# Attention's output in a fused macaron kernel: division on GpSimd, early value chunks and an early attention share, output products that accumulate both parts

## The chip, the cores and the metric

The kernel runs on one core of one Trainium2 chip. The metric is the device time of one execution in microseconds. A core has four engines that compute (TensorE, VectorE, ScalarE, GpSimd) and a queue that only issues transfers (SyncE); each works through its own list of instructions in order, and semaphores tie the lists together. In the rows below they are PE (PEld is its loading of weights), DVE, ACT, POOL and SP.

## What is computed

The reference has three stages on x of 4 batches x 1024 tokens x 128 channels: a local-attention stack of two layers, one global attention with a line memory, and the same local stack again. The change is in the end of the middle stage:

```python
attn = jax.nn.softmax(scores, axis=-1)
seq_out = jnp.einsum('bhts,bhsd->bhtd', attn, v)
...
mem_val = x @ memv_w.T + memv_b
gate = jax.nn.sigmoid(x @ memg_w.T + memg_b)
mem_score_t = jnp.transpose(mem_score, (0, 2, 1))
gated = jax.nn.sigmoid(mem_score_t * mem_scale) * gate
gated = jnp.mean(gated, axis=-1, keepdims=True)
return (seq_out + gated * mem_val) @ out_w.T + out_b
```

`x` in these lines is the normalised input, `y` in the kernel; the result is added to the residual stream, `x` in the kernel. All of this is fp32.

## The kernel before

`macaron_kernel` runs a setup pass, `local_attention_pass`, `global_attention_pass` and `local_attention_pass` again. A barrier of all engines stands between two passes, so the second local pass starts when the slowest engine of the global pass is through. All tensors are laid with channels on the partitions and tokens along the row.

**The global pass** ends with the line memory, a loop over 8 tiles of 128 tokens (`body(t)` in each engine's list, t = 0 to 7, all four batches at once). For tile t TensorE makes `memory(t, 0)` to `memory(t, 5)` (16 heads of 144 columns, line 1821), into three PSUM banks in turn; VectorE multiplies each bank by the read lines (`terms`, 2044), sums (`read_memory`, 2054), and makes the score of the tile in three steps (`weigh`, 2062, 2066, 2070); TensorE turns the score to rows (`turn`, 1830), and ScalarE copies it out (`copy_scores`, 2396). In tiles 0 to 5 TensorE also makes the lines of tile t + 2; tiles 6 and 7 have none, so they are short. Tile 6 is `body(LAST - 1)`, tile 7 is `body(LAST)`; `turn(6)` is the last step of `body(7)`, and `turn(7)` is all of `body(8)`.

**The output stage** works on 8 chunks of 512 tokens; chunk i is batch i % 4, half i // 4. For each chunk:

- `memory_value` (1857): memv x y, one fp32 product of 128x512; ScalarE adds the bias (`value_bias`, 2410).
- the spread inverse of the softmax's sums, a product of 32 rows (1873), and the spread mean of the gate, a product of 16 rows (1879). `inverse_and_mean(pair)` makes both for two chunks: four products on four different quarters of TensorE's rows.
- VectorE: `scale_seq` (2106) is the attention's sum times the inverse, `gate_value` (2113) the value times the mean.
- GpSimd: `combine` (2309) adds the two.
- TensorE: `back` (1885), out_w x the combined chunk, one product; VectorE adds the bias and the residual (`back`, 2121).

The gate needs, once for each half, `gates` (1844, four products of 16 columns side by side), two sigmoids on ScalarE (2399, 2404) and a product on GpSimd (`gate_product`, 2302). Half 1 needs the scores of all tiles, and with them `turn(7)`.

The order is written out by hand in each list. On TensorE: `gates(0)`, `gates(1)`, `memory_value(0)` and `(1)` after tile 6; `inverse_and_mean(0)` inside tile 7; `memory_value(2)` and `(3)` behind it; and the rest behind `turn(7)`. The banks of lines and tails (M0 to M0 + 2, O0) are free from tile 6 on, the memory's banks (S0 to S0 + 3) after tile 7.

## Time and profile before

| | us |
|---|---|
| median of 3 runs | 1919.88 (1919.46 to 1920.75) |
| profiled execution | 1922.61 |
| its span, first to last instruction | 1920.7 |
| tiles 6 and 7, `memory(6, 3)` to `turn(7)` | 1228.24 to 1243.01 |
| `turn(7)` to the last VectorE instruction of the stage | 1243.01 to 1264.55 |

The rows that stand further down come from this one profiled execution. Times in them are counted from the start of its span. A matmul in fp32 leaves two records in the trace, so a product of 128x512 is "x2" there. A row of the timeline merges neighbours of one kind: its duration runs from the start of the first record to the end of the last.

### The profile page before, as it was taken

The numbers are of one execution on the slowest core, as the hardware profiler recorded it, in microseconds if no ns is written. First come the engines' busy times: TensorE is split into PE (matmuls) and PEld (weight loads), VectorE is DVE, ScalarE is ACT, GpSimd is POOL, SyncE is SP. The second block draws the span as 40 slices with busy tenths as digits, with TensorE's granted clock in tenths as the row PEclk, the third lists the DMA queues.
The fourth block names the chain that finished last, engine by engine and source line by source line (L and its number), as shares of the span: only waits on it lengthen the run. The fifth ranks groups of instructions, "written<-read, shape, count | busy, mean of one in ns | idle before, by whom it ended". The sixth has DMA issues, their size and how long they took to land. (4 is left out here: it accounts for less than half of the span.)

```text
span 1920.7 us, 61287 instructions
## 1 busy us (share of the span) xinstructions
PE 1856.6 (97%) x22646; PEld 1108.6 (58%) x22646; DVE 1603.5 (83%) x5443; ACT 1491.9 (78%) x4110; POOL 929.2 (48%) x568
## 2 busy tenths in 40 slices
PE   7999999999999989999999999889999999999999
PEld 3777774577775443344444448637777635777754
DVE  5899974899995668999999949979999658999945
ACT  4999995699998362777777763469999847999973
POOL 2788861488883050000000036648888405888820
PEclk9999999999999995999999999999999999999999
DMA  6212230122221041111111000002121201222211
GB/s 179 50 44 50 45 70 6 29 47 48 47 54 42 1 151 38 42 41 41 42 41 41 26 7 5 2 20 51 44 51 44 62 6 36 45 50 45 67 23 44
DMA packets 76330, 85.33 MB, mean 44 GB/s; under 512 B 17327, under 2 KB 50803, under 8 KB 75907
## 3 DMA queue, kind: packets, MB, share of 16 engines
q1 hardware_dynamic: 75839, 81.40, 17.0%
q8 instruction: 182, 2.98, 0.7%
q14 instruction: 113, 0.93, 0.2%
q10 hardware_dynamic: 196, 0.02, 0.0%
HBM read 20.83 MB, written 8.39 MB: 15 GB/s over the span
## 5 line engine op out<-in xcount | busy, mean ns | idle before, releaser
L336 ACT ACTIVATE probs<-probs,negmax 128x128 f32<-128x128 f32 x1024 | 401.9, 402 | 2.3 <-DVE negmax L411 1.9
L2328 ACT ACTIVATE gprobs<-ps_global 128x1024 f32<-128x1024 f32 (+3 forms) x384 | 291.5, 811 | 126.2 <-PE ps_global L1765 103.5
L291 POOL TENSOR_TENSOR rot<-rot 128x1024 f32<-128x1024 f32 x128 | 302.5, 2363 | 143.9 <-DVE rot L381 143.9
L297 POOL TENSOR_TENSOR qk<-rot,cnorm 128x1024 f32<-128x1024 f32 x128 | 244.0, 1906 | 173.6 <-issue 150.9
L304 POOL TENSOR_TENSOR probs<-probs,iden 128x1024 f32<-128x1024 f32 x128 | 243.0, 1898 | 47.2 <-DVE iden L419 46.5
L2010 DVE TENSOR_REDUCE maxes<-ps_global 128x1 f32<-128x512 f32 (+2 forms) x384 | 222.1, 639 | 11.6 <-PE ps_global L1728 6.5
L411 DVE CUSTOM_DVE_ANT_0 probs<-ps_attn,masks 128x128 f32<-128x128 f32 x1024 | 226.2, 287 | 0.8 <-issue 0.8
L336 ACT ACTIVATION_READ_ACCUMULATOR probs<-probs,negmax 128x1 f32 x1024 | 204.2, 199 | 0.0
L1723 PE MATMUL ps_global<-kq 48*128 48x512 bf16 (+3 forms) x768 | 197.3, 346 | 7.1 <-DVE maxes L2010 1.8
L2240 POOL CAST m_parts<-m_turn 32x128 bf16<-32x128 f32 x16 | 4.5, 282 | 364.7 <-DVE m_turn L2024 364.7
L377 DVE TENSOR_TENSOR rot<-ps_attn,rotary 128x512 f32<-128x512 f32 x256 | 175.1, 684 | 1.8 <-PE ps_attn L202 1.5
L1780 PE MATMUL ps_global<-gprobs,v_all 128*9 128x512 f32 (+3 forms) x1536 | 161.3, 492 | 1.0 <-ACT gprobs L2328 1.0
L271 PEld LDWEIGHTS ps_attn<-probsT,v_first 128*64 128x64 f32 x2048 | 103.8, 137 | 97.7 <-ACT probsT L357 93.9
L255 PEld LDWEIGHTS ps_attn<-ident,probs 128*128 128x128 f32 x1024 | 120.4, 142 | 67.0 <-issue 64.6
L638 ACT ACTIVATE ln<-ps_attn,vecs_sb 128x512 f32<-128x512 f32 (+2 forms) x96 | 65.6, 684 | 115.7 <-PE ps_attn L600 71.6
L387 DVE TENSOR_REDUCE ssq<-sq 128x16 f32<-128x1024 f32 x128 | 154.8, 1209 | 0.1
L2006 DVE CUSTOM_DVE_ANT_0 ps_global<-ps_global,later 128x384 f32<-128x384 f32 (+1 forms) x256 | 152.2, 653 | 2.7 <-PE ps_global L1723 0.6
L1723 PEld LDWEIGHTS ps_global<-kq 48*128 48x128 bf16 x768 | 58.9, 94 | 160.7 <-DVE maxes L2010 86.9
L224 PE MATMUL ps_attn<-ident,qk 128*128 128x128 f32 x1024 | 141.3, 281 | 7.2 <-POOL qk L297 4.4
L1756 PE MATMUL ps_global<-kq 51*128 51x512 bf16 (+3 forms) x768 | 145.6, 330 | 2.7 <-ACT gprobs L2328 1.9
L282 PE MATMUL ps_attn<-oT,wo_sb 128*128 128x128 f32 x1024 | 135.3, 275 | 0.0
L255 PE MATMUL ps_attn<-ident,probs 128*128 128x128 f32 x1024 | 133.6, 274 | 0.6 <-POOL probs L304 0.6
(235 smaller groups left out, 4501.5 us busy)
## 6 DMA issues: line engine op xcount, KB each, us to landing
v_first<-v_second SPq DMA_DIRECT2D x256, 128.0 KB, 2.3
hs<-z_a SPq DMA_DIRECT2D x256, 32.0 KB, 1.9
ln<-z_b SPq DMA_DIRECT2D x56, 128.0 KB, 2.4
kq<-split_scratch SPq DMA_DIRECT2D x64, 96.0 KB
kq<-split_scratch SPq DMA_DIRECT2D x64, 64.0 KB
split_scratch<-parts SPq DMA_DIRECT2D x8, 384.0 KB, 4.3
split_scratch<-gprobs SPq DMA_DIRECT2D x6, 384.0 KB, 4.0
x_tok<-in_x_dram SPq DMA_DIRECT2D x4, 512.0 KB, 5.8
```

What stands on the lines that cost most here:

```text
L255: last = nc.tensor.transpose(ps[:, b, s * TILE:(s + 1) * TILE], probs[:, k % 2, 4 * e + s, :], K["ident"][:, :])
L291: nc.gpsimd.tensor_tensor(a, a, b, ALU.add).then_inc(C["rot_sum"], 1)
L297: nc.gpsimd.tensor_tensor(qk[:, k % 2, :].rearrange("p (h d) -> p h d", d=DH), rot_a[:, k % 2, :, :], cnorm[:, k % 2, :].unsqueeze(2).to_b ...
L304: nc.gpsimd.tensor_tensor(pr, pr, iden[:, k % 2, :].unsqueeze(2).to_broadcast([P, HEADS, SPAN]), ALU.mult).then_inc(C["probs_ready"], 1)
L336: last = nc.scalar.activation(probs[:, k % 2, slot, :], probs[:, k % 2, slot, :], ACT.Exp, scale=-1.0, bias=negmax[:, k % 2, slot:slot + 1 ...
L377: nc.vector.tensor_tensor(rot_a[:, k % 2, h0:h0 + HEADS, :], x, cos, ALU.mult)
L387: nc.vector.reduce_sum(ssq[:, k % 2, :], sq[:, :].rearrange("p (h d) -> p h d", d=DH), AX_X).then_inc(C["ssq_done"], 1)
L411: nc.vector.tensor_tensor_reduce(probs[:, k % 2, slot, :], ps[:, SB0 + slot // 4, (slot % 4) * SPAN:(slot % 4 + 1) * SPAN], K["masks"][:, ...
L1723: mm = nc.tensor.matmul(out, qs[buf][rows, p, tile_cols(t)], ks[buf][rows, p, CHUNK * c:CHUNK * c + w], start=True, stop=not masked_here, ...
L1780: mm = nc.tensor.matmul(ps[32 * h:32 * h + AD + 1, O0, t0 - CHUNK * c:CHUNK], v_all[:, S_TILES * (n // GROUPS) + s, GROUP * (n % GROUPS) + ...
L2010: nc.vector.reduce_max(maxes[:, n % 2, r, p0:p1, t, c], ps[:, bank_of(use), 0:len(both) * w].rearrange("q (p s) -> q p s", s=w), AX_X).the ...
L2328: nc.scalar.activation(probs[:, step % RING, 2 * p:2 * p + 2, 0:w], ps[:, S0 + 2 * p:S0 + 2 * p + 2, 0:w], ACT.Exp).then_inc(C["p2_exp"], 1)
```

## The change

Per chunk the arithmetic is split differently. GpSimd multiplies the attention's sum by the spread inverse in place (`divide_attention`), after ScalarE has copied that inverse out of PSUM (`copy_inverse`), since GpSimd works on SBUF. `combine` and `scale_seq` are gone. The two parts meet in PSUM instead: `out_w` is multiplied with the divided attention and with the gated value separately.

- For chunks 0 to 3 `attention_part` makes out_w x attention plus identity x residual, and ScalarE writes the sum with the bias to x (`attention_sum`); `back` is then one product, and VectorE adds it to x.
- For chunks 4 to 7 `back` makes out_w x attention and out_w x gated value in one bank; chunks 5 and 7 add identity x residual there too, and ScalarE writes them (`late_sum`).

The inverses are spread in pairs of their own (`inverse_spread`), and the means of a half in one group of four (`means`). A list of 22 names, `EARLY`, gives the order in which the four free banks are used; "V0" is the value of chunk 0, "I" an inverse, "G" a gate, "X" an attention part.

```diff
+        EARLY = ("V0", "V1", "I0", "I1", "V2", "V3", "G0", "G1", "I2", "I3", "I4", "I5", "V4", "V5", "X0", "X1", "I6", "I7",
+                 "X2", "X3", "V6", "V7")
+        FREED = (M0, M0 + 1, M0 + 2, O0)
...
+            def await_early(kind, i):
+                n = early(kind, i)
...
+                wait(pe, "oo_taken", n - 3)
...
+            def inverse_spread(i):
+                b, half = batch_half(i)
+                first = 32 * ((b + 2) % B)
+                await_early("I", i)
...
+                nc.tensor.matmul(ps[:, early_bank("I", i), :], A["head_spread"][first:first + 32, half, :], iden[first:first + 32, :],
+                                 start=True, stop=True, tile_position=(first, 0)).then_inc(C["oo_early"], 1)
...
+            def attention_part(i):
+                await_early("X", i)
+                wait(pe, "oo_norm", i + 1)
+                nc.tensor.matmul(ps[:, early_bank("X", i), :], A["out_w"][:, :], chunk_of(o_all, i), start=True, stop=False)
+                nc.tensor.matmul(ps[:, early_bank("X", i), :], K["ident"][:, :], chunk_of(x, i), start=False, stop=True
+                                 ).then_inc(C["oo_early"], 1)
+
+            def means(half):
+                wait(pe, "oo_prod", half + 1)
+                if half == 0:
                     wait(pe, "ml_term", USES_M * S_TILES)
...
+                for b in range(B):
+                    mm = nc.tensor.matmul(ps[:, mean_bank(b), :], A["head_mean"][32 * b:32 * b + AH, :],
+                                          prod[32 * b:32 * b + AH, half, :], start=True, stop=True, tile_position=(32 * b, 0))
+                mm.then_inc(C["oo_mean"], 1)
...
             def back(i):
-                wait(pe, "oo_comb", i + 1)
-                nc.tensor.matmul(ps[:, inverse_bank(i), :], A["out_w"][:, :], comb[:, i % 2, :], start=True, stop=True
-                                 ).then_inc(C["oo_proj"], 1)
+                await_back_bank(i)
+                out = ps[:, back_bank(i), :]
+                if i < B:
+                    wait(pe, "oo_gated", i + 1)
+                    nc.tensor.matmul(out, A["out_w"][:, :], gated_of(i), start=True, stop=True).then_inc(C["oo_proj"], 1)
+                    return
+                wait(pe, "oo_norm", i + 1)
+                nc.tensor.matmul(out, A["out_w"][:, :], chunk_of(o_all, i), start=True, stop=False)
+                if i in LATE_SUMS:
+                    nc.tensor.matmul(out, K["ident"][:, :], chunk_of(x, i), start=False, stop=False)
+                wait(pe, "oo_gated", i + 1)
+                nc.tensor.matmul(out, A["out_w"][:, :], gated_of(i), start=False, stop=True).then_inc(C["oo_proj"], 1)
...
+            def divide_attention(i):
+                wait(gp, "oo_taken", early("I", i) + 1)
+                nc.gpsimd.tensor_tensor(chunk_of(o_all, i), chunk_of(o_all, i), inverse_of(i), ALU.mult).then_inc(C["oo_norm"], 1)
...
+            def copy_inverse(i):
+                wait(act, "oo_early", early("I", i) + 1)
+                wait(act, "oo_norm", i - 3)
...
+                nc.scalar.copy(inverse_of(i), ps[:, early_bank("I", i), :]).then_inc(C["oo_taken"], 1)
```

VectorE now runs `gate_value` for chunks 0 to 3, `back` 0 to 2, `gate_value` 4 to 7, then `back` 3, 4 and 6. GpSimd divides chunks 0 to 3 behind tile 7's lines, makes `gate_product(0)`, divides 4 to 7, and makes `gate_product(1)`. ScalarE's order from tile 6 on: `copy_scores(4)`, values 0 and 1, `scale_lines(6)`, inverses 0 and 1, values 2 and 3, the first half's sigmoid and both gate sigmoids, inverses 2 and 3, `copy_scores(5)`, inverses 4 and 5, values 4 and 5, `scale_lines(7)`, attention sums 0 and 1, inverses 6 and 7, attention sums 2 and 3, `copy_scores(6)`, values 6 and 7, `copy_scores(7)`, the second half's sigmoid, and the sums of chunks 5 and 7.

TensorE's list between `turn(5)` (16x128 from gprobs) and tile 7's first memory product (v_all, decay), before:

```order
L1830 MATMUL ps_global<-ident,gprobs 16x128 x3
L1844 MATMUL ps_global<-z_a,memg_sb 16x512 [waits ml_state,ml_mul]
L1844 MATMUL ps_global<-z_a,memg_sb 16x512 x7
L1857 MATMUL ps_global<-z_a,memv_sb 128x512 x2
L1821 MATMUL ps_global<-v_all,decay 128x144 [waits ml_term,ml_row1]
```

And now:

```order
L1844 MATMUL ps_global<-ident,gprobs 16x128 x3
L1862 MATMUL ps_global<-z_a,memv_sb 128x512 [waits oo_taken] x2
L1878 MATMUL ps_global<-z_a,memg_sb 16x512 [waits oo_taken]
L1878 MATMUL ps_global<-z_a,memg_sb 16x512 x3
L1878 MATMUL ps_global<-z_a,memg_sb 16x512 [waits oo_taken]
L1878 MATMUL ps_global<-z_a,memg_sb 16x512 x3
L1871 MATMUL ps_global<-later,head_spread_sb 128x512 [waits oo_taken] x2
L1835 MATMUL ps_global<-v_all,decay 128x144 [waits ml_term,ml_row1]
```

A pair of spread inverses now stands there beside two values (chunks 2 and 3; values 0 and 1 moved up into tile 6, with another pair of inverses).

TensorE's list from `turn(6)` to the first `back`, before (`turn(7)` is the second row of ident, gprobs that waits):

```order
L1830 MATMUL ps_global<-ident,gprobs 16x128 [waits ml_out,ml_score]
L1830 MATMUL ps_global<-ident,gprobs 16x128 x3
L1857 MATMUL ps_global<-z_a,memv_sb 128x512 [waits ml_term]
L1857 MATMUL ps_global<-z_a,memv_sb 128x512
L1830 MATMUL ps_global<-ident,gprobs 16x128 [waits ml_out,ml_score]
L1830 MATMUL ps_global<-ident,gprobs 16x128 x3
L1873 MATMUL ps_global<-later,head_spread_sb 128x512 [waits oo_prod,ml_out,oo_stage,oo_value]
```

And now, from behind `turn(6)`:

```order
L1885 MATMUL ps_global<-z_b,out_w_sb 128x512 [waits oo_norm,oo_taken]
L1886 MATMUL ps_global<-x_sb,ident 128x512
L1885 MATMUL ps_global<-z_b,out_w_sb 128x512 [waits oo_norm,oo_taken]
L1886 MATMUL ps_global<-x_sb,ident 128x512
L1871 MATMUL ps_global<-later,head_spread_sb 128x512 [waits oo_taken] x2
...
L1862 MATMUL ps_global<-z_a,memv_sb 128x512 [waits oo_taken]
L1897 MATMUL ps_global<-v_all,head_mean_sb 128x512 [waits ml_out,ml_term,oo_prod]
L1897 MATMUL ps_global<-v_all,head_mean_sb 128x512 x3
L1862 MATMUL ps_global<-z_a,memv_sb 128x512 [waits oo_taken]
L1844 MATMUL ps_global<-ident,gprobs 16x128 [waits ml_out,ml_score,oo_taken]
```

Two values stood between the two turns; now there are eight products of the attention parts (four shown), two values, a pair of inverses and the first half's means.

The end of TensorE's list in this stage, before:

```order
L1873 MATMUL ps_global<-later,head_spread_sb 128x512 [waits oo_prod,oo_x,oo_stage,oo_value]
L1873 MATMUL ps_global<-later,head_spread_sb 128x512
L1879 MATMUL ps_global<-v_all,head_mean_sb 128x512 x2
L1885 MATMUL ps_global<-kq,out_w_sb 128x512 [waits oo_comb] x4
```

And now, behind `means(1)` (chunks 2 and 3 first):

```order
L1916 MATMUL ps_global<-kq,out_w_sb 128x512 [waits oo_gated,oo_taken]
L1916 MATMUL ps_global<-kq,out_w_sb 128x512 [waits oo_gated,ml_out]
L1919 MATMUL ps_global<-z_b,out_w_sb 128x512 [waits oo_norm,oo_x]
L1923 MATMUL ps_global<-o_cols,out_w_sb 128x512 [waits oo_gated]
L1919 MATMUL ps_global<-z_b,out_w_sb 128x512 [waits oo_norm,oo_x]
L1921 MATMUL ps_global<-x_sb,ident 128x512
L1923 MATMUL ps_global<-o_cols,out_w_sb 128x512 [waits oo_gated]
L1919 MATMUL ps_global<-z_b,out_w_sb 128x512 [waits oo_norm,oo_x]
L1923 MATMUL ps_global<-kq,out_w_sb 128x512 [waits oo_gated]
L1919 MATMUL ps_global<-z_b,out_w_sb 128x512 [waits oo_norm,oo_gated]
L1921 MATMUL ps_global<-x_sb,ident 128x512
L1923 MATMUL ps_global<-kq,out_w_sb 128x512 [waits oo_gated]
```

Behind the last means stood four products of 128x512; now there are twelve, ten of them for chunks 4 to 7.

## Rows read from the trace of the kernel before

**Rows 1.** The page: busy time of each engine over the span
```profile
PE 1856.6 (97%) x22646; PEld 1108.6 (58%) x22646; DVE 1603.5 (83%) x5443; ACT 1491.9 (78%) x4110; POOL 929.2 (48%) x568
```

**Rows 2.** Stretches: length, busy time per engine (records), granted PE clock, DMA
```profile
core 0: us, PE busy (x) PEld busy (x) DVE busy (x) ACT busy (x) POOL busy (x), PEclk, DMA share, GB/s
1228.24:1264.55 36.31, 30.30 (x150) 14.06 (x150) 29.89 (x45) 10.63 (x19) 16.25 (x13) 0.95 0.00 1
1243.01:1247.27 4.26, 3.54 (x19) 1.31 (x20) 4.13 (x7) 0.99 (x2) 2.44 (x2) 0.71 0.00 0
1247.27:1264.55 17.28, 13.29 (x39) 4.50 (x37) 11.47 (x17) 2.75 (x4) 8.77 (x8) 0.97 0.00 0
```

**Rows 3.** Timeline of TensorE, tiles 6 and 7: start, duration, [idle before <-releaser]
```profile
1228.24 1.98 PE L1821 MATMUL ps_global<-v_all,decay 128*128 128x144 f32 x14 [2.32 <-DVE kq L2044]
1230.16 0.41 PE L1830 MATMUL ps_global<-ident,gprobs 128*16 128x128 f32 x8
1230.39 1.90 PE L1844 MATMUL ps_global<-z_a,memg_sb 128*16 128x512 f32 x16
1232.22 1.98 PE L1857 MATMUL ps_global<-z_a,memv_sb 128*128 128x512 f32 x4
1234.04 2.37 PE L1821 MATMUL ps_global<-v_all,decay 128*128 128x144 f32 x18
1236.34 0.70 PE L1873 MATMUL ps_global<-later,head_spread_sb 32*128 32x512 f32 x2
...
1237.41 1.98 PE L1821 MATMUL ps_global<-v_all,decay 128*128 128x144 f32 x14
1239.32 0.41 PE L1830 MATMUL ps_global<-ident,gprobs 128*16 128x128 f32 x8
1239.94 1.99 PE L1857 MATMUL ps_global<-z_a,memv_sb 128*128 128x512 f32 x4 [0.21 <-DVE kq L2044]
```

**Rows 4.** Timeline of TensorE behind tile 7
```profile
1243.01 0.41 PE L1830 MATMUL ps_global<-ident,gprobs 128*16 128x128 f32 x8 [1.09 <-DVE gprobs L2070]
...
1245.40 2.08 PE L1857 MATMUL ps_global<-z_a,memv_sb 128*128 128x512 f32 x2 [0.24 <-DVE kq L2113]
1247.27 2.35 PE L1885 MATMUL ps_global<-kq,out_w_sb 128*128 128x512 f32 x4
...
1254.15 1.88 PE L1885 MATMUL ps_global<-kq,out_w_sb 128*128 128x512 f32 x4
1256.96 0.70 PE L1873 MATMUL ps_global<-later,head_spread_sb 32*128 32x512 f32 x2 [0.93 <-DVE x_sb L2121]
...
1261.41 2.35 PE L1885 MATMUL ps_global<-kq,out_w_sb 128*128 128x512 f32 x4 [1.40 <-POOL kq L2309]
```

**Rows 5.** Timeline of VectorE: `weigh` of tile 7, and the stage's last instruction
```profile
1242.40 0.55 DVE L2070 TENSOR_REDUCE gprobs<-gprobs 128x64 f32<-128x384 f32 x1
...
1263.80 0.75 DVE L2121 SCALAR_TENSOR_TENSOR x_sb<-ps_global,out_bias,x_sb 128x512 f32<-128x512 f32 x1 [0.47 <-PE ps_global L1885]
```

**Rows 6.** Single lines: duration of one record in ns, min/median/max
```profile
L1821 PE MATMUL ps_global<-v_all,decay x46: 286/286/391, 1228.2 to 1239.1; 128*128 128x144 f32 x46
L1885 PE MATMUL ps_global<-kq,out_w_sb x16: 592/592/1061, 1247.3 to 1263.2; 128*128 128x512 f32 x16
L2410 ACT ACTIVATE v_all<-ps_global,attn_cols x8: 687/687/689, 1233.4 to 1254.3; 128x512 f32<-128x512 f32 x8
L2399 ACT ACTIVATE parts<-gprobs,attn_cols x2: 722/722/723, 1230.8 to 1243.8; 128x512 f32<-128x512 f32 x2
L2302 POOL TENSOR_TENSOR v_all<-parts x2: 1272/1273/1274, 1232.3 to 1247.3; 128x512 f32<-128x512 f32 x2
L2113 DVE TENSOR_TENSOR kq<-v_all,ps_global x8: 680/681/689, 1244.1 to 1259.9; 128x512 f32<-128x512 f32 x8
```

**Rows 7.** Timelines of GpSimd and of ScalarE: last step of tile 7's lines; score copy
```profile
1231.22 0.87 POOL L2269 TENSOR_TENSOR parts<-kq 128x384 f32<-128x384 f32 x1
...
1243.49 0.27 ACT L2396 COPY gprobs<-ps_global 128x128 f32<-128x128 f32 x1 [0.84 <-PE ps_global L1830]
```

More of the change, by code:

```diff
@@ L1860, in inverse_and_mean @@
-            def inverse_and_mean(pair):
-                wait(pe, "oo_value", (2, 4, 6, 8)[pair])
-                wait(pe, "oo_stage", 2 + 2 * 16)
-                wait(pe, "oo_prod", 1 + pair // 2)
-                if pair == 0:
-                    wait(pe, "oo_sig", 3)
-                elif pair == 1:
+                    mm = nc.tensor.matmul(ps[32 * b:32 * b + AH, early_bank("G", half), :], A["memg"][:, :], y[:, c:c + CHUNK],
+                                          start=True, stop=True, skip_group_check=True, tile_position=(0, 32 * b))
@@ L1867, in inverse_and_mean, with await_back_bank @@
+            def await_back_bank(i):
+                if i < 3:
+                    wait(pe, "oo_taken", len(EARLY) - 2 + i)
+                elif i == 3:
                     wait(pe, "ml_out", S_TILES)
-                else:
-                    wait(pe, "oo_x", 2 * pair - 2)
-                for i in (2 * pair, 2 * pair + 1):
-                    b, half = batch_half(i)
-                    first = 32 * ((b + 2) % B)
-                    mm = nc.tensor.matmul(ps[:, inverse_bank(i), :], A["head_spread"][first:first + 32, half, :],
-                                          iden[first:first + 32, :], start=True, stop=True, tile_position=(first, 0))
@@ L1875, in inverse_and_mean @@
-                mm.then_inc(C["oo_turned"], 1)
-                for i in (2 * pair, 2 * pair + 1):
-                    b, half = batch_half(i)
-                    first = 32 * b
-                    mm = nc.tensor.matmul(ps[:, mean_bank(i), :], A["head_mean"][first:first + AH, :],
-                                          prod[first:first + AH, half, :], start=True, stop=True, tile_position=(first, 0))
-                mm.then_inc(C["oo_mean"], 1)
-            def back(i):
-                wait(pe, "oo_comb", i + 1)
-                nc.tensor.matmul(ps[:, inverse_bank(i), :], A["out_w"][:, :], comb[:, i % 2, :], start=True, stop=True
-                                 ).then_inc(C["oo_proj"], 1)
+                elif i < CHUNKS - 1:
+                    wait(pe, "oo_x", i - 3)
+                else:
+                    wait(pe, "oo_gated", B + 1)
@@ L1962, in _ @@
                 body(t)
-            memory_value(2)
-            memory_value(3)
+            attention_part(0)
+            attention_part(1)
+            inverse_spread(6)
+            inverse_spread(7)
+            attention_part(2)
+            attention_part(3)
+            memory_value(6)
+            means(0)
+            memory_value(7)
+            wait(pe, "oo_taken", len(EARLY) - 3)
             body(S_TILES)
-            inverse_and_mean(1)
-            memory_value(4)
             back(0)
             back(1)
-            memory_value(5)
-            inverse_and_mean(2)
-            memory_value(6)
-            memory_value(7)
-            back(2)
-            back(3)
-            inverse_and_mean(3)
-            for i in range(4, CHUNKS):
+            means(1)
+            for i in range(2, CHUNKS):
                 back(i)
@@ L2208, in _ @@
                     nc.vector.reciprocal(den_late[:, :], den_late[:, :]).then_inc(C["oo_in"], 1)
-            for pair in range(GROUPS):
-                chunks = (2 * pair, 2 * pair + 1)
-                if pair >= 2:
-                    for i in chunks:
-                        back(i - 4)
-                for i in chunks:
-                    scale_seq(i)
-                for i in chunks:
-                    gate_value(i)
-            for i in range(4, CHUNKS):
-                back(i)
+            for i in range(B):
+                gate_value(i)
+            for i in range(3):
+                back(i)
+            for i in range(B, CHUNKS):
+                gate_value(i)
+            for i in range(3, CHUNKS):
+                if i not in LATE_SUMS:
+                    back(i)
         @block.gpsimd
```

207 lines of the change are left out of this document (121 added, 86 removed).

## The prediction

> **What bounds the kernel now.** I read the page first: TensorE is busy for 97% of the span [rows 1], so the first question to an edit is what it adds to TensorE. The stage that is changed is one stretch of 36.31 us, from `memory(6, 3)` at 1228.24 to VectorE's last instruction, which starts at 1263.80 and ends at 1264.55 [rows 2, 3, 5]. Behind it stands a barrier, so its end moves everything later by as much. Next I read the timeline of each engine there. In tiles 6 and 7 VectorE sets the pace up to the last score, 1242.40 + 0.55 = 1242.95 [rows 5], and `turn(7)` follows at 1243.01 [rows 4]; TensorE waits 0.21 and 1.09 us for it [rows 3, 4], and has one hole of 2.32 us just before 1228.24 [rows 3]. Behind 1243.01 the work is handed round between TensorE, VectorE, GpSimd and ScalarE, and TensorE waits at each round, 0.93 and 1.40 us at two of them [rows 4]. The granted clock is 0.71 of full in 1243.01 to 1247.27 and 0.97 in the rest [rows 2]: part of that time is at the lower level (1.2 GHz), behind a stretch in which TensorE had waited.
>
> **The price of TensorE's work.** One record of 128x512 lasts 0.59 us, and a run of four lasts 1.88 [rows 4, 6], so they follow each other by (1.88 - 0.59) / 3 = 0.43, and an fp32 product (two records) takes 0.86. A record of the memory lasts 0.286, and 18 take 2.37 [rows 3, 6]: (2.37 - 0.29) / 17 = 0.122 each. 18 of them make 2.20, but the next group starts 2.30 after their first [rows 3]: a change of shape costs about 0.1. The group of four 32- and 16-row products holds TensorE from 1236.34 to 1237.41, 1.07 us, 1.27 with a change before and behind it. A pair alone is not in the trace. Its bounds are 1.07 (each of its records still streams 512 columns, twice, side by side on other rows, as in the group of four) and the 1.72 of two products one after the other; I take 1.27 with the changes. `turn` is 0.23 (1230.16 to 1230.39), 0.45 with its changes; two `gates` are 1.83, 1.92 with theirs [rows 3].
>
> **TensorE's list before,** from 1228.24: 8 values and 8 `back` 13.76; four groups 5.08; gates 1.92; 46 memory records 5.64; three turns 1.35. Together 27.75 us of 36.31. The other 8.6 are the sum behind the last product (about 0.9), the lower clock (0.29 x 4.26 + 0.03 x 17.28 = 1.7 [rows 2]) and some 6 us of waits.
>
> **TensorE's list after.** Values 0 and 1 (1.72) fit in the 2.32 us hole before 1228.24 and cost nothing: the lines of tile 7 are multiplied by then, and the banks are free. From 1228.24 on:
>
> - six values, 6 x 0.86 = 5.16; gates 1.92; memory 5.64; turns 1.35: 14.07, as before less two values.
> - four pairs of inverses, 5.08, and two groups of means, 2.54: 7.62 where there were 5.08.
> - attention parts of chunks 0 to 3, two products each, one of them only to add the residual: 8 x 0.86 = 6.88, new.
> - `back`: 4 products for chunks 0 to 3, 2 + 3 + 2 + 3 for chunks 4 to 7: 14 x 0.86 = 12.04 where there were 6.88.
>
> That is 40.6 us, 12.9 more. It replaces work on VectorE (eight `scale_seq`) and the eight adds on GpSimd; neither saves TensorE anything.
>
> **Its waits after.** I laid the four lists beside each other with these durations. TensorE goes through tiles 6 and 7 without waiting: net, 6.0 us more stand there (four values more and three pairs, less the group of four: 3.44 + 3.81 - 1.27), against 0.2 us of waits before. `turn(5)` ends at 1231.8, two values, the gates and a pair follow, and tile 7's first memory product starts at 1236.7 instead of 1234.04, which VectorE now waits for (1.9 us). `turn(6)` is at 1243.6 instead of 1239.32. Attention parts, inverses 6 and 7 and value 6 run to 1253.0. Two waits remain. At `means(0)` ScalarE has to sum chunk 3 (0.69 [rows 6]) and copy score 6 (0.27 [rows 7]) beside one product (0.86): 0.3 with the hand-overs. At `means(1)`: `turn(7)` at 1255.6, then value 7 on ScalarE until 1256.5, the score copy 0.27, the sigmoid 0.72, the gate's product on GpSimd 1.27 [rows 6, 7], so 1258.7; `back` 0 and 1 cover 1.72 of it, and 1.0 is waited. From there twelve products, 10.3, run without a gap: the gated values of chunks 4 to 7 are four VectorE instructions of 0.68 [rows 6], ready before their turn. The sum is 1228.24 + 0.1 + 40.6 + 1.3 = 1270.2 for TensorE, and 0.9 for the end of the last product and its sum on ScalarE (0.69 [rows 6]): 1271.2.
>
> The other engines are far from binding. ScalarE has 32 instructions of at most 0.72 us in these 43 us. GpSimd has eight divisions and two gate products; for one of them the nearest row is the 1.27 of 128x512 [rows 6]. That is 12.7 us, it can begin at 1231.22 + 0.87 = 1232.1 [rows 7], and what is queued behind the divisions of chunks 0 to 3 there is only `gate_product(0)`, needed at 1253. A division could be held up or lengthened while VectorE reads, by up to its own length; four of them even at twice the price end before the attention parts need them but for one or two, so I take 0 and put 1.3 as the upper bound.
>
> **The sum.** 1271.2 - 1264.55 = 6.7 us more. The profiled execution took 1922.61 with a span of 1920.7, so its like would take 1929.3; the median of the runs is 2.73 lower, 1919.88 + 6.7 = **1926.6**. The bounds: with changes of shape free (14 of them, 1.4) and the waits gone (1.3), 1923.9; with a pair of inverses at 1.72, 2.6 more, and a late division, 1.3, 1930.5. I hold the lower half likelier, because four products on four row quarters did run beside each other.
>
> **Rivals.**
>
> *The early work hides, and the time is not measurably longer.* In tiles 6 and 7 TensorE follows VectorE, so what is put there might not move `turn(6)` from 1239.3. For it: VectorE has no gap there, and there is the hole of 2.32 us. Against it: TensorE's own rows run edge to edge from 1228.24 to 1239.7 [rows 3], so 6.0 us of products have no room. It decides at tile 7's first memory product. If that one stays at 1234.0, 4.3 us fall out: 1922.3.
>
> *Products into an open bank cost half* (the other side). The 18 products of attention parts and of `back` 4 to 7 share banks in twos and threes; if the second record of one ran beside the first of the next, as products on different row quarters do, 18 x 0.43 = 7.7 us would go: 1918.9. It decides if two accumulating products start 0.43 apart. Against it: they use all 128 rows, and the products of that kind in the trace are 0.86 apart whatever their bank.
>
> *The lower clock again.* Before `means(1)` TensorE waits 1.0 us, and its clock fell once already behind waits [rows 2]. As long a stretch at the lower level costs the same 1.7 us: 1928.3.
>
> *The waits close and the added products lie in them.* The 6 us of waits and the 1.7 of lower clock go and nothing comes for them: 1912.2. Against it stand the 12.9 us of added products, twice the waits there are. The Trainium skill, Perfetto Trace Analysis, Optimization Strategies, says the aim is to keep the matmul engine as highly used as possible; a reader who goes by that would expect this case, since TensorE's use rises from 27.75 of 36.3 us to 40.6 of 43. The rows speak against the rule here: what rises is its work, not its work per microsecond saved.
>
> **How the numbers follow.** The forecast 0.78, the lower clock 0.09, the hidden work 0.07, the half price 0.03, the closed waits 0.02, and 0.01 for something else. About 0.2% (3.8 us) is what a measurement of this kernel can tell from no change. Slower by more means above 1923.7: nearly all of the first two, 0.86. Within: the hidden work, the half price, a little of the forecast's low end, 0.11. Faster: 0.03. The range of 8 in 10 is 1923.6 to 1929.0: it leaves out the cases on the other side (0.13 together) and the far end of the unknown prices.
>
> **What would show it.** Right: `turn(6)` near 1243.6, `turn(7)` near 1255.6, `means(1)` near 1258.7 behind a wait for GpSimd, twelve products without a gap behind it, a last sum on ScalarE that ends near 1271, and TensorE's idle time in the stage down from 6 to under 2 us. Wrong: a pair of inverses much off 1.07, accumulating products closer than 0.86, tile 7's first memory product at 1234, or a wait for a division or for ScalarE of more than 1 us among the attention parts. If the start of the second local pass moves by less than the stage's end, the barrier does not pass the loss on.

## The result, and the profile after

The changed kernel took 1923.88 us, the median of 10 runs (1921.54 to 1925.56); the kernel before, run beside it, 1919.67 (10 runs, 1915.69 to 1920.94). The ratio is 1.0024, 95% interval 1.0015 to 1.0033: slower by 4.6 us, between 2.9 and 6.3 (the two medians are 4.2 apart). The profiled execution took 1924.29, with a span of 1922.2 and a granted clock of 0.987.

The two spans differ by 1.5 us only, and half of what hides the rest lies ahead of the change: the changed kernel reaches the stage 2.52 us earlier in its trace. A stretch at half clock at about 719 us, in code that is the same in both, lasts 37.55 us there instead of 40.96, and small waits differ in number. So I count from a zero that both have, the first record of `memory(6, 3)`: 1228.24 before [rows 3], 1225.72 after.

TensorE's timeline of the changed kernel in the stage (start, duration, [idle before <-releaser]; the rows that answer to [rows 3, 4]):

```profile
1225.72 1.49 PE L1835 MATMUL ps_global<-v_all,decay 128*128 128x144 f32 x10 [0.60 <-DVE kq L2093]
1227.15 1.13 PE L1871 MATMUL ps_global<-later,head_spread_sb 32*128 32x512 f32 x4
1228.20 0.76 PE L1835 MATMUL ps_global<-v_all,decay 128*128 128x144 f32 x4
1228.89 0.41 PE L1844 MATMUL ps_global<-ident,gprobs 128*16 128x128 f32 x8
...
1234.05 2.47 PE L1835 MATMUL ps_global<-v_all,decay 128*128 128x144 f32 x18
1236.45 1.13 PE L1871 MATMUL ps_global<-later,head_spread_sb 32*128 32x512 f32 x4
1237.51 1.49 PE L1835 MATMUL ps_global<-v_all,decay 128*128 128x144 f32 x10
...
1241.14 0.41 PE L1844 MATMUL ps_global<-ident,gprobs 128*16 128x128 f32 x8
...
1250.89 1.14 PE L1897 MATMUL ps_global<-v_all,head_mean_sb 16*128 16x512 f32 x8 [0.17 <-ACT gprobs L2434]
1251.96 1.13 PE L1862 MATMUL ps_global<-z_a,memv_sb 128*128 128x512 f32 x2
1253.02 0.41 PE L1844 MATMUL ps_global<-ident,gprobs 128*16 128x128 f32 x8
1253.36 1.98 PE L1916 MATMUL ps_global<-o_cols,out_w_sb 128*128 128x512 f32 x4
1256.12 1.14 PE L1897 MATMUL ps_global<-v_all,head_mean_sb 16*128 16x512 f32 x8 [0.78 <-POOL v_all L2341]
1257.19 1.98 PE L1916 MATMUL ps_global<-kq,out_w_sb 128*128 128x512 f32 x4
1259.02 1.02 PE L1919 MATMUL ps_global<-z_b,out_w_sb 128*128 128x512 f32 x2
1259.88 1.02 PE L1923 MATMUL ps_global<-o_cols,out_w_sb 128*128 128x512 f32 x2
...
1266.74 1.02 PE L1923 MATMUL ps_global<-kq,out_w_sb 128*128 128x512 f32 x2
```

TensorE waits twice behind 1226, 0.17 and 0.78 us, where it waited again and again before. Over the whole span its share of busy time says nothing of this, 97% as in [rows 1]:

```profile
PE 1868.4 (97%) x22674; PEld 1114.1 (58%) x22674; DVE 1597.9 (83%) x5433; ACT 1499.3 (78%) x4124; POOL 928.4 (48%) x568
```
The windows (length, busy time and records per engine, granted clock, DMA) say the same, to be read against [rows 2]:

```profile
1226.00:1243.00 17.00, 17.00 (x102) 9.32 (x102) 13.18 (x19) 10.58 (x20) 11.62 (x10) 1.00 0.01 2
1243.00:1269.00 26.00, 23.82 (x74) 8.95 (x72) 10.74 (x18) 7.85 (x14) 3.83 (x4) 1.00 0.00 0
```

17.00 of 17.00 us busy, and the granted clock is full throughout; the trace of before has a stretch at 0.71. The others now wait for TensorE, VectorE even in tile 7, and ScalarE makes the last sum; before, VectorE did [rows 5]:

```profile
1235.16 2.01 DVE L2093 TENSOR_TENSOR kq<-ps_global,parts 128x432 f32<-128x432 f32 x3 [1.69 <-PE ps_global L1835]
1241.24 0.46 DVE L2093 TENSOR_TENSOR kq<-ps_global,parts 128x288 f32<-128x288 f32 x1 [1.66 <-PE ps_global L1835]
1252.09 1.28 DVE L2154 TENSOR_TENSOR o_cols<-gprobs,ps_global 128x512 f32<-128x512 f32 x2 [7.32 <-PE ps_global L1897]
1267.80 0.69 ACT L2464 ACTIVATE x_sb<-ps_global,out_bias 128x512 f32<-128x512 f32 x1 [3.60 <-PE ps_global L1923]
```

Counted from the zero, in us (the forecast's absolute times less 1228.24):

| place | before | forecast | after |
|---|---|---|---|
| tile 7's first memory product | 5.80 | 8.5 | 8.33 |
| `turn(6)` | 11.08 | 15.4 | 15.42 |
| `turn(7)` | 14.77 | 27.4 | 27.30 |
| `means(1)` | – | 30.5 | 30.40 |
| end of the last sum | 36.31 | 43.0 | 42.77 |

The stage is 6.46 us longer where 6.7 was forecast. The first product of the second local pass follows 0.85 us behind the stage before and 0.84 after, so the barrier passes all of it on. Yet the time rose by 4.6. In the traces the second pass gives some back: from its first product to the end it takes 655.3 us before, 652.9 after.

### The profile page after: what moved, and what is told of

Read it like the earlier page. It is cut to its first block and busy times, and to the rows that moved or that the text cites. A ratio compares the mean times of both kernels' runs of the same rounds, so it can differ in the third digit from the quotient of the medians.

```text
span 1922.2 us, 61344 instructions
## 1 busy us (share of the span) xinstructions
PE 1868.4 (97%) x22674; PEld 1114.1 (58%) x22674; DVE 1597.9 (83%) x5433; ACT 1499.3 (78%) x4124; POOL 928.4 (48%) x568
```

## Experiments

Two theories at first. **A:** the stage is set by TensorE's list, product by product, and its length is the whole difference. **B:** the second pass is really shorter behind a longer stage and gives some back. "Stage" is from ScalarE's sigmoid table load to the last write of x: 37.20 us before, 43.65 after. In the expectations "the kernel before" is the one of the trace ahead of the prediction.

**The changed kernel once more,** unedited:

> The changed kernel once more, nothing edited. Stage here and below: from ScalarE's load of the sigmoid table (tile 6) to the last write of x in the global pass; 37.19 us before (1227.36 to 1264.55), 43.65 after (1224.84 to 1268.49), so the stage itself lost 6.46, while the whole moved by 4.2 (medians of 10). Theory A: the stage is set by TensorE's list and repeats within 0.1 us: 43.6 to 43.8; what lies ahead of and behind the stage differs from trace to trace by 2 to 3 us for reasons outside the change, so the ratio can lie anywhere in 1.0020 to 1.0035. Theory B: the second local pass is itself shorter behind the change by 2.4 us (655.3 before, 652.9 after, from its first TensorE product): then it is again 652.9 here, and the ratio is 1.0020 to 1.0025.

Measured: 1925.45 (before beside it 1920.77, 32 runs), ratio 1.0024 (1.0014 to 1.0034). Stage 43.65, second pass 653.5. Both findings repeat.

**The early products of tile 7 moved behind it.** Inverses 4 and 5 and values 4 and 5 follow `turn(6)`, and ScalarE scales tile 7's lines ahead of their copies.

```
-                elif t == LAST:
-                    inverse_spread(4)
-                    inverse_spread(5)
...
-                elif t == LAST:
-                    memory_value(4)
-                    memory_value(5)
...
+            inverse_spread(4)
+            inverse_spread(5)
+            memory_value(4)
+            memory_value(5)
```

> The changed kernel with inverses 4 and 5 and values 4 and 5 moved out of tile 7 to just behind turn(6); ScalarE scales tile 7's lines ahead of their copies. TensorE's total work is the same, tile 7 gets its 3.0 us back. Theory A (TensorE's list sets the end, wherever its products stand): stage 43.4 to 43.9, no change in time beyond 0.5 us. Rival (the 1.7 + 1.7 us that VectorE waits in tile 7 set the end): VectorE's last score comes 3 us earlier and the stage shrinks to about 40.5, time 3 us down, ratio to before about 1.0008.

Measured: 1925.39, ratio 1.0022 (1.0013 to 1.0031), stage 43.46. VectorE's two waits in tile 7 are no loss of their own: the same products at another place cost the same.

**The identity products taken out.** ScalarE copies the attention share, GpSimd adds it to x for chunks 0 to 3, and VectorE makes all last sums.

```
-                nc.tensor.matmul(ps[:, early_bank("X", i), :], K["ident"][:, :], chunk_of(x, i), start=False, stop=True
...
-        LATE_SUMS = (5, 7)
+        LATE_SUMS = ()
...
+            def add_share(i):
+                wait(gp, "oo_taken", early("X", i) + 1)
+                nc.gpsimd.tensor_tensor(chunk_of(x, i), chunk_of(x, i), chunk_of(o_all, i), ALU.add).then_inc(C["oo_late"], 1)
```

> The changed kernel without its six products by the identity. GpSimd adds ScalarE's copy of the attention share (kept in the attention's own buffer) to x for chunks 0 to 3, VectorE adds bias and residual for chunks 4 to 7. Theory A: each product was 0.86 us on the path: stage 43.65 - 5.16 = 38.5 (38.2 to 39.2, a wait for GpSimd's adds may open), time 5.2 us under the changed kernel, 1.3 over the one before, ratio to before 1.000 to 1.001. Rival (hand-overs set the end, products hide): stage over 42.

Measured: 1922.66, ratio 1.0009 (1.0001 to 1.0018). Stage 38.57: six products of 0.86 are 5.16, and 5.08 went. The first and the last of its output products, and VectorE's last sum:

```profile
1257.67 1.02 PE L1918 MATMUL ps_global<-z_b,out_w_sb 128*128 128x512 f32 x2
...
1263.68 1.02 PE L1922 MATMUL ps_global<-kq,out_w_sb 128*128 128x512 f32 x2
1264.74 0.75 DVE L2162 SCALAR_TENSOR_TENSOR x_sb<-ps_global,out_bias,x_sb 128x512 f32<-128x512 f32 x1 [0.97 <-PE ps_global L1922]
```

TensorE's products stand 0.86 apart to the end, without a wait. So the six products that only add the residual make up 5.08 of the 6.5 to 7.6 us that the change costs the stage.

**The sum made first.** The gated value and the attention output are added (even chunks on GpSimd, odd ones on VectorE), and one product per chunk follows: 14 products fewer than in the changed kernel, with its early values, inverses and divisions kept.

```
-                nc.tensor.matmul(out, A["out_w"][:, :], gated_of(i), start=False, stop=True).then_inc(C["oo_proj"], 1)
+                wait(pe, "oo_part" if i % 2 else "oo_late", i // 2 + 1)
+                nc.tensor.matmul(out, A["out_w"][:, :], gated_of(i), start=True, stop=True).then_inc(C["oo_proj"], 1)
...
+                nc.vector.tensor_tensor(gated_of(i), gated_of(i), chunk_of(o_all, i), ALU.add).then_inc(C["oo_part"], 1)
```

> Division on GpSimd and all value chunks early, as in the change, but gated value and attention are added before the product (even chunks on GpSimd, odd on VectorE), and each chunk has one product by out_w: 14 products of 128x512 fewer than the changed kernel, 12.0 us of TensorE's work; no attention parts, no identity products. Theory A: TensorE stops being the bound behind tile 7; VectorE's list of eight gated values, four adds and eight sums (5.3 + 2.3 + 5.5, 13 us) and the gate's chain set the end: stage 32 to 34.5, time 3 to 5 us under the kernel before, ratio 0.997 to 0.9985. Rival (the new hand-overs between GpSimd, ScalarE and TensorE cost as much as the old ones): stage 37 or more, ratio 1.000 or over.

Measured: 1919.59, ratio 0.9993 (0.9984 to 1.0001), stage 35.08. It is shorter than before but misses the 34.5, and the ratio misses the expected 0.997 to 0.9985. VectorE has become the bound: its list runs without a gap. Where one of its additions starts while GpSimd's is running, it takes 1.02 to 1.19. The one of 0.69 also lies beside GpSimd's: the two start within 0.01 us of each other, and there it is GpSimd's that took longer, 1.81 instead of 1.09. TensorE waited 1.19 and 2.60 us and was then at half clock just behind the stage: 3.4 us of the window below are at 1.2 GHz. VectorE's timeline, GpSimd's, then a window of 4 us at the start of the second pass:

```profile
1246.60 1.02 DVE L2238 TENSOR_TENSOR o_cols<-o_cols,z_b 128x512 f32<-128x512 f32 x1
1247.54 1.27 DVE L2142 TENSOR_TENSOR kq<-gprobs,ps_global 128x512 f32<-128x512 f32 x2
1248.91 0.69 DVE L2238 TENSOR_TENSOR kq<-kq,z_b 128x512 f32<-128x512 f32 x1
...
1255.19 1.19 DVE L2238 TENSOR_TENSOR kq<-kq,z_b 128x512 f32<-128x512 f32 x1
1256.31 3.37 DVE L2147 SCALAR_TENSOR_TENSOR x_sb<-ps_global,out_bias,x_sb 128x512 f32<-128x512 f32 x5
```
```profile
1245.97 1.09 POOL L2353 TENSOR_TENSOR o_cols<-o_cols,z_b 128x512 f32<-128x512 f32 x1
...
1248.92 1.81 POOL L2353 TENSOR_TENSOR kq<-kq,z_b 128x512 f32<-128x512 f32 x1
...
1254.57 1.26 POOL L2353 TENSOR_TENSOR kq<-kq,z_b 128x512 f32<-128x512 f32 x1 [1.88 <-DVE kq L2142]
```
```profile
1260.50:1264.50 4.00, 3.97 (x6) 1.63 (x7) 0.00 (x0) 1.65 (x3) 0.00 (x0) 0.57 0.00 0
```

So A stands for the stage. The second pass is another matter: 656.6 us in the kernel without identity products and 658.3 in this one. The next six runs are about that.

**The kernel before once more:**

> The kernel before, unedited, for a second trace of it. Measured from ScalarE's sigmoid table load to the last write of x, the stage took 37.20 us in the first trace, and the second pass (its first TensorE product to the end) 655.3. Theory A (the second pass costs the same wherever it starts, up to scatter): the new trace shows 37.2, and a second pass anywhere between the 652.9 of the changed kernel and 656.6. Theory B (the second pass is really shorter behind the changed kernel's longer stage): 37.2 and 655.3 within 0.3 again.

Measured: ratio 0.9999 (0.999 to 1.0008). The second pass took 656.4, so it is again longer than in the changed kernel, by 2.9 to 3.6 us, and not the 655.3 within 0.3 that theory B asked for. The stage took 36.08 instead of 37.20, since the stretch at half clock is absent. The window that answers to the 0.71 of [rows 2]:

```profile
1241.67:1245.93 4.26, 3.42 (x20) 1.14 (x20) 4.13 (x7) 1.67 (x3) 2.44 (x2) 1.00 0.00 0
```

That stretch comes in some executions and not in others, and costs the stage 1.12 us. That is less than the 1.7 that half clock takes from TensorE's own work; that the rest lies in its waits is an inference. The change's cost to the stage is therefore 6.46 beside one trace of before and 7.57 beside the other.

**A delay on TensorE** behind the last output product of the kernel before:

```
+            wait(pe, "oo_x", 5)
+            for _ in range(8):
+                nc.tensor.matmul(ps[:, inverse_bank(4), :], A["out_w"][:, :], comb[:, 0, :], start=True, stop=True)
```

> The kernel before with eight unused 128x512 products more behind the last output product: TensorE is busy for 8 x 0.86 = 6.9 us more, of which 0.8 lie beside the last sum, so the second pass starts 6.1 us later, about as late as in the changed kernel. Nothing else is altered. Theory A: the time rises by the whole 6.1, ratio 1.0032 (1926.9 beside 1920.8). Theory B: the second pass gives back 2.0 to 2.4 us, ratio 1.0020 (1924.7), and its PE rows show the gain at about 1508 to 1520 us of the trace, as in the changed kernel.

**The same delay on ScalarE,** TensorE idle:

```
+            wait(act, "oo_x", CHUNKS)
+            for k in range(9):
+                wait(act, "oo_pad", k)
+                nc.scalar.copy(value_of(0), value_of(2)).then_inc(C["oo_pad"], 1)
```

> The kernel before with nine unused 128x512 copies on ScalarE behind the last sum, 0.60 to 0.70 us each: the second pass starts 5.4 to 6.3 us later, this time with TensorE idle meanwhile. Theory A: +5.4 to +6.3, ratio 1.0028 to 1.0033; a half-clock stretch right behind the idle time (as one follows the 2.6 us of idle in the kernel with the sum made first) would add 1.7 more, 1.0041. Theory B (what counts is when the second pass starts): the same 2.0 to 2.4 given back as behind the TensorE delay, 1.0017 to 1.0021.

Measured: 1925.83, ratio 1.0021 (1.0012 to 1.003), and 1927.37, ratio 1.0035 (1.0023 to 1.0048, from five runs), beside 1920.81. In both the second pass starts 6.1 to 6.3 us behind VectorE's last sum instead of 0.28. By the ratios the delay on TensorE cost 4.0 us (2.3 to 5.8) and the one on ScalarE 6.7 (4.4 to 9.2). The intervals overlap, so it is not shown that the first gave 2 us back and the second nothing.

The two profiled executions took 1929.26 and 1931.63, 3 to 4 us more than their medians, and have two stretches at half clock inside the stage, ahead of the added instructions. Up to the last write of x the stage took 38.9 us in both, where 36.08 is the length without such a stretch. Two windows of the delay on TensorE:

```profile
1228.00:1232.00 4.00, 4.00 (x30) 2.19 (x32) 3.93 (x6) 1.07 (x2) 2.92 (x3) 0.57 0.03 6
1245.00:1249.00 4.00, 3.65 (x12) 1.49 (x5) 3.37 (x6) 0.75 (x2) 3.63 (x3) 0.57 0.00 0
```

TensorE's second pass, counted alike, is 654.0 and 657.9. The pass behind the delay on ScalarE has a stretch of half clock at its start. Laid record by record beside the changed kernel's, it loses 2.0 us in its first 23 us and 2.4 us around a stop that is described below. The two passes start at 1272.07 and 1271.90, so it isn't the time at which the pass starts, as theory B had it.

What tells them apart is in TensorE's timeline at line 242, a group of 32 small products, 64 records, in the second pass. The second trace of before, then the changed kernel padded (below), then before padded with 14 products:

```profile
1515.30 0.98 PE L242 MATMUL ps_attn<-kT,qT 64*32 64x96 f32 x62
1517.29 0.35 PE L242 MATMUL ps_attn<-kT,qT 64*32 64x96 f32 x2 [1.01 <-issue]
```
```profile
1522.49 0.96 PE L242 MATMUL ps_attn<-kT,qT 64*32 64x96 f32 x61
1524.20 0.35 PE L242 MATMUL ps_attn<-kT,qT 64*32 64x96 f32 x3 [0.75 <-issue]
```
```profile
1514.68 1.00 PE L242 MATMUL ps_attn<-kT,qT 64*32 64x96 f32 x64
```

TensorE stops for 1 us within the group and waits for nothing that the profile shows. Its instructions are loaded meanwhile, in transfers of 16 KB on a DMA queue of their own; the page counts them (before, then after):

```profile
q8 instruction: 182, 2.98, 0.7%
```
```profile
q8 instruction: 183, 3.00, 0.7%
```

TensorE has 45,292 matmul and weight-load records in the kernel before, 46,754 with waits and drains: 182.6 times 256, so one transfer holds about 256 instructions. In the traces with the stop, a transfer starts 0.17 to 0.93 us ahead of the group; in the traces without, the nearest ones start 3.0 us or more ahead of it and 1.0 to 2.0 us behind its start. This goes together in all fourteen traces; that the transfer is the cause is not shown. **Theory C:** the stop goes with the place of the instructions in TensorE's stream, which every added product moves. **Theory D:** chance, or the pass's start.

```
+                if t == LAST - 1:
+                    wait(pe, "ml_term", USES_M * t - 2)
+                    for _ in range(14):
+                        nc.tensor.matmul(ps[0:32, MEMORY + USES_M * t % 3, 0:1], K["ident"][:, 0:32], K["ident"][:, 0:1], start=True, stop=True)
                 memories(0, 3)
```

> In both traces of the kernel before, TensorE stands still for 1.01 us within a group of 64 small products of the second pass (line 242), with no wait there, at its matmul record 18110 of 22646; one of its instruction loads (16 KB, queue q8) is under way there. The trace of the kernel with the ScalarE delay (22646 records too) and of the one with the sum made first (22646) show the same stall; the changed kernel (22674), the TensorE delay (22662), the kernel without identity products (22662) and the mixed one (22650) do not. Here the kernel before gets 14 unused one-column products (28 records) into TensorE's wait of 2.32 us in tile 6, so that its later instructions lie where those of the changed kernel lie. Nothing that the stage needs is moved. Theory C (the stall goes with the place of the instructions in TensorE's stream): the stall at line 242 is gone, the second pass takes 652.9 to 654.3 us instead of 655.3 and 656.4, and the time falls by 1.0 to 2.4 us, ratio 0.9987 to 0.9995. Theory D (the stall goes with when the second pass starts, or is chance): the stall is there, 655 to 656.5, ratio 1.0.

Measured: the stop is gone, the second pass takes 653.4, the stage 36.07. It starts at 1263.41 and the pass of 656.4 at 1262.96, which speaks against the start time once more. But the time doesn't show the gain: ratio 0.9998 (0.9989 to 1.0006), the median 1.1 us lower (1917.84 beside 1918.94), where 0.9987 to 0.9995 was expected.

In the next two, products of the same kind stand at the start of the global pass, 64 in the kernel before and 49 in the changed one:

```
             for m in range(2):
                 variance(m)
+            for _ in range(64):
+                nc.tensor.matmul(ps[0:32, 0, 8:9], K["ident"][:, 0:32], K["ident"][:, 0:1], start=True, stop=True)
```

> The kernel before with 64 unused one-column products (128 matmul and 128 weight-load records: 256 instructions, as many as one 16 KB load of 64 bytes each) at the start of the global pass, some 550 us ahead of the stall. Theory C: the later instructions lie in the loads as before, and the stall of 1.0 us is again within the group of line 242, at record 18238 of 22774. Theory D gives no reason for either. The pads cost 1 to 5 us, ratio 1.0005 to 1.0026.

> The changed kernel with 49 unused one-column products (98 matmul and 98 weight-load records) at the start of the global pass. With its own 28 and 28 more and 5 more waits that makes 257 instructions ahead of the place in question, one load and one instruction, the offset that the kernel with the sum made first has. Theory C: the stall of 1.0 us at line 242 of the second pass is there, the second pass takes 654.5 to 656.5 instead of 652.9 and 653.5, and the time rises above the changed kernel's by the pads (1 to 4 us) and by 1.0 to 2.4 for the stall: ratio 1.0035 to 1.0055. Theory D: no stall there, as in both traces of the changed kernel, ratio 1.003 to 1.0045.

Measured: ratio 1.0033 (1.0021 to 1.0045) and 1.0067 (1.0054 to 1.0079), both above what was expected (1.0005 to 1.0026 and at most 1.0055). The executions of each lie in two groups some 5 us apart (three at 1921.4 to 1922.0 and four at 1926.5 to 1927.5; two at 1927.0 to 1927.5 and four at 1931.2 to 1933.8). The traces are of 1921.35 and 1927.52, so they don't show what makes the difference, and it stays open. In the first trace the 64 pads ran 5.06 us. In the changed kernel the stop came, 0.75 us long, at the place that C implies: record 18235 of 22772, which is 18109, its place in the kernel with the sum made first, and the 126 records added ahead of it. The second pass grew from 652.9 and 653.5 to 655.3. In the kernel before it did not stay, though the stream was moved by one whole transfer: 653.1. C's cycle of one transfer is wrong; transfers start there 2.97 us ahead of the group and 1.77 behind its start, which a shift by 256 instructions alone does not give.

| kernel | matmul records | stage | second pass | stop at L242 |
|---|---|---|---|---|
| before, two traces | 22646 | 37.20, 36.08 | 655.3, 656.4 | 1.01 |
| delay on ScalarE | 22646 | 38.88 | 657.9 | 1.01 |
| sum made first | 22646 | 35.08 | 658.3 | 1.02 |
| changed, 49 pads | 22772 | 43.65 | 655.3 | 0.75 |
| before, 14 pads | 22674 | 36.07 | 653.4 | none |
| before, 64 pads | 22774 | 36.08 | 653.1 | none |
| delay on TensorE | 22662 | 38.89 | 654.0 | none |
| changed, two traces | 22674 | 43.65, 43.65 | 652.9, 653.5 | none |
| products moved behind tile 7 | 22674 | 43.46 | 653.5 | none |
| no identity products | 22662 | 38.57 | 656.6 | none |
| mixed, two versions (below) | 22650, 22648 | 34.41, 33.79 | 653.8, 653.9 | none |

Without the stop the second pass took 652.9 to 654.0, with one exception; with it, 655.3 to 658.3, the two longest with half clock at their start. The stop is 1.0 of these 2 to 3 us. Another 0.9 goes a few us ahead of it, where TensorE waits 1.19 us for GpSimd's line 297 in the first trace of before and 0.32 in the changed kernel's. Laid record by record beside the first trace of the changed kernel, the traces with the stop lose 2.1 to 2.4 us between 243 and 258 us into the pass (1.6 with the stop of 0.75), and all others at most 0.13 there. The exception, without identity products, loses 3.7 us elsewhere, 2.8 of them in the last 250 us of the pass.

**A version that keeps the early work and drops the added products.** The sum made first, but for chunk 7, whose attention part and gated value share a bank as in the changed kernel; its x once by an identity product, once on VectorE. The products of chunk 7 stand ahead of those of chunk 6:

```
+                if i == CHUNKS - 1:
+                    nc.tensor.matmul(out, A["out_w"][:, :], chunk_of(o_all, i), start=True, stop=False)
+                    nc.tensor.matmul(out, K["ident"][:, :], chunk_of(x, i), start=False, stop=False)
```

> The kernel in which value and attention are added first and one product follows, with its last chunk taken back to the changed kernel's way: for chunk 7 three products in one bank (attention, x by the identity, gated value) and ScalarE's sum with the bias. VectorE was busy without a gap from the scores at 1245.22 to the end at 1259.68 there; it loses one addition (1.19 us beside GpSimd's) and one sum (0.67), TensorE gains two products (1.7) that fit into its waits of 0.65 and 1.19. Theory A: VectorE's list ends at about 1257.8, the stage takes 33.0 to 33.9 us instead of 35.08, and the time is 3.3 to 4.2 below the kernel before, ratio 0.9978 to 0.9983. Rival: TensorE's list, now 11 products and the means from 1247.2, is as long as VectorE's, and the stage stays at 34.5 to 35.1, ratio 0.9985 to 0.999. With theory B the second pass is longer by 1 to 3 us the earlier it starts, and the ratio stays at 0.999 whatever the stage does.

The second version is the same without the last line; VectorE makes chunk 7's sum in ScalarE's place, ahead of chunk 6's.

> The mixed kernel without the identity product of chunk 7, whose sum VectorE makes again. In its trace TensorE's list ended last: 10 products of 0.86 and the identity behind each other from 1253.55, and VectorE waited 1.20 for the last one. Expected: TensorE ends 0.86 earlier, VectorE makes two sums behind it, of which one overlaps the last product, and the stage takes 33.4 to 33.8 us instead of 34.41; the time 4.5 to 5.5 below the kernel before, ratio 0.9971 to 0.9977. Rival: VectorE's list, one sum longer and already 16.0 us busy of 18.0, takes back what TensorE gives, and the stage stays at 34.2 to 34.5, ratio 0.9979. Its 22648 records leave open whether the stall at line 242 is there; if so, 1.0 us more.

Measured: 1917.23 beside 1920.81, ratio 0.9979 (0.9969 to 0.9988), stage 34.41; and 1914.96 beside 1918.94, ratio 0.9981 (0.9973 to 0.999), stage 33.79. The first stage is nearly the rival's 34.5: TensorE's list ended last. The second stage fell by 0.62, as expected, and VectorE's list now closes it without a gap. Its ratio stayed above the expected 0.9971 to 0.9977, so the time does not show that gain. TensorE's last products, and VectorE's:

```profile
1256.64 1.88 PE L1920 MATMUL ps_global<-kq,out_w_sb 128*128 128x512 f32 x4
```
```profile
1254.97 1.27 DVE L2149 TENSOR_TENSOR kq<-kq,ps_global 128x512 f32<-128x512 f32 x2
1256.16 3.37 DVE L2154 SCALAR_TENSOR_TENSOR x_sb<-ps_global,out_bias,x_sb 128x512 f32<-128x512 f32 x5
```

By their ratios both beat the kernel before by some 4 us and the changed one by some 8.

## Why the prediction was right, and where it was off

- **Direction and size.** 1926.6 was forecast beside a median of 1919.88, +6.7; measured +4.6 (2.9 to 6.3). The time, 1923.88, lies 0.28 us above the lower end of the range (1923.6). It got that low by something that the forecast had put at nothing (the last point), so that it still lies inside is in part luck; the stage's length is not.
- **The price of a product, 0.86.** Right in two ways: the open-bank products follow each other by 0.86 (1259.02, 1259.88), and taking six out gave 5.08. The rival of half price falls. Its own 7.7 us was too much besides: by its condition only neighbours in one bank overlap, ten pairs among the 18 products, so 4.3 us.
- **A pair of inverses, assumed at 1.07 plus changes.** A pair's four records hold TensorE from 1236.45 to 1237.51: 1.06. The far bound of 1.72 is out.
- **Values 0 and 1 in the hole of 2.32.** Right: the wait there is 0.60.
- **No room in tiles 6 and 7.** Right: tile 7's memory starts at 8.33 (forecast 8.5), and moving four products out of the tile changed nothing. The rival of hidden work falls. One figure of this step is miscounted: "6.0 us more" takes values 2 and 3 as new ahead of `turn(6)` without taking off values 0 and 1, which stood there before. Two values and three pairs, less the group of four, are 1.72 + 3.81 - 1.27 = 4.3. The forecast of `turn(6)` goes by that, and 15.42 - 11.08 = 4.34 was measured.
- **The two waits behind.** Forecast 0.3 and 1.0, measured 0.17 and 0.78.
- **The other engines.** The eight divisions were put at 1.27 each and took 1.09 to 1.29, and TensorE waited for none. One term was missed and cost nothing: VectorE's line 2111 took 1.53 us in tile 6 beside two divisions, 0.62 in tile 7.
- **The lower clock.** The rival of a new stretch at half clock did not come: no stretch in the stage in three of three traces of the changed kernel, the padded one among them. The forecast read the old one as 1.7 us of the stage; two traces of before put it at 1.12.
- **Waits that close.** TensorE's idle time in the stage did go from 6.0 us to 1.7 (from 5.2 to 1.0 without the end behind its last product), as that rival would have it, and the stage got longer by the products. The Trainium skill (Perfetto Trace Analysis, Optimization Strategies) gives as the goal to keep the matmul engine as highly used as possible; by that measure alone the changed kernel would be the better one, and it is the slower. The mixed version shows the other side: less TensorE work than in the changed kernel, more waits, faster.
- **The step that failed** is the last of the sum: the stage's loss was carried to the end whole, "its end moves everything later by as much". The barrier did pass it on, and the second pass gave 2.5 back. By the two pairs of traces, 6.45 - 2.47 = 4.0 and 7.57 - 2.92 = 4.65, which is the measured size.

What that 2.5 is, is settled in part. Shown: it is not the start time of the pass; 2.1 us of it go in 15 us of the pass, around a stop of 1.0 us; this stop comes and goes with instructions added far ahead of it, and the second pass is 2 to 3 us shorter without it in all kernels but one. Not shown: what causes the stop, and that the time follows. Removing the stop alone gave 0.4 us less (0.9998, from 2.1 less to 1.2 more) where 1.0 to 2.4 was expected; the interval holds both no gain and most of the expected one. Another part may be the clock. Where the changed kernel was run again, its mean granted clock over the runs was 0.9868, that of before 0.9857; the runs with at least 0.987 alone, 7 and 6 of them, have medians of 1925.23 and 1919.22, 6.0 us apart. I read this off the runs afterwards and made no experiment for it; the two accounts overlap, and how they share the 2 us stays open.

## What to carry to other kernels

In a stretch where the bound engine already does most of the work, count its products before and after, times their spacing: that sum, with two waits, gave the stage to 0.3 us. Two products into one bank save an addition elsewhere and cost a product here. Moving work early into idle time and adding work to the bound engine are separate edits; here the first (with one or two products added) was worth 4 us, and the rest of the products cost twice that.

Behind a stage, do not expect a loss or gain to arrive whole when only 0.2% is at stake: stops and stretches of half clock come and go elsewhere in the kernel, the stop hundreds of us behind the added instructions, and take 1 to 3 us. Judge the stage by its own trace, the kernel by many runs.

## What the runs showed of the hardware

- TensorE's instructions arrive in transfers of 16 KB, about 256 instructions (182 transfers, 46,754 records). In a group of 64 records that follow each other by 12 ns ((1.00 - 0.24) / 63, one record being 0.24 us long) TensorE stopped for 0.75 to 1.02 us in five traces of fourteen, those in which such a transfer had started at most 0.93 us before the group. The cause is not shown.
- Four records of 32 rows on two quarters of the array take 1.06 us, as long as the four products of both kinds together took [rows 3] (1.07): a lone pair leaves the other two quarters unused.
- VectorE and GpSimd hold each other up. VectorE's addition of 128x512 took 1.02 to 1.19 us where it started while a GpSimd addition was running, and ended 0.55 us after that one each time. Where the two started within 0.01 us of each other, VectorE's took 0.69 and GpSimd's 1.81 instead of 1.09. A 128x384 operation on VectorE took 0.62, and 1.53 beside two divisions.
- One-column fp32 products with 32 columns of weights took 5.06 us for 64, 79 ns each (part of it at half clock), far more than the 24 ns (two records) of the small products at line 242.
